# Preparing adj, weights and biases as pieces of the list schedule, in a four-layer graph network on one core

## The reference, cut to what matters

```python
x = layernorm(x + L0(x))   # D^-1/2 adj D^-1/2 (x @ w0) + b0, D = row sums of adj
x = layernorm(x + L1(x))   # 8-head attention masked by adj == 0; o = proj(...) + b; o + layernorm(o)
x = layernorm(x + L2(x))   # 3 GRU steps: a = adj @ h; z, r, candidate from a and h by w3, w4, w5, u3, u5
x = layernorm(x + L3(x))   # 8-head attention, scores + (1 - adj) * -1e9; Wq, Wk, Wv, Wo with biases
```

## Time and profile before

| | |
|---|---|
| device time, median of 3 runs | 2658.07 us (2657.05 to 2658.81) |
| device time of the profiled execution | 2658.25 us |
| its span in the trace | 2656.5 us |
| busy: PE, DVE, ACT, POOL | 97%, 74%, 72%, 27% of the span |
| granted TensorE clock, mean | 0.991 |
| HBM traffic | 14.36 MB read, 8.39 MB written |

### The profile page before, as it was taken

The page is one execution under the profiler, slowest core; times in us unless marked ns, Lnnn a source line. Parts: engine busy times, 40 slices in busy tenths (PEclk is TensorE's granted clock), DMA queues, the critical chain, the costliest instruction groups (busy, mean ns, idle before and its releaser), DMA issues.

```text
span 2656.5 us, 50191 instructions
## 1 busy us (share of the span) xinstructions
PE 2576.8 (97%) x17448; PEld 2056.3 (77%) x17448; DVE 1962.5 (74%) x5499; ACT 1904.9 (72%) x4284; POOL 715.1 (27%) x1065
## 2 busy tenths in 40 slices
PE   4999999999999999999999999999999999999997
PEld 3877877787877878778787787878777787777875
DVE  5867867868587786867768587685877868676776
ACT  2767947768587775858768587685867859574777
POOL 1222141322313222132322313223132321413221
PEclk7999999999999999999999999999999999999999
DMA  3312212122031221203122121221302113021122
GB/s 114 72 25 49 49 29 60 41 48 49 24 77 29 53 45 46 67 17 72 33 51 54 26 63 41 48 49 40 68 22 58 39 44 69 17 49 24 26 62 58
DMA packets 85081, 126.68 MB, mean 48 GB/s; under 512 B 15264, under 2 KB 34144, under 8 KB 84832
## 3 DMA queue, kind: packets, MB, share of 16 engines
q1 hardware_dynamic: 84832, 123.47, 19.7%
HBM read 14.36 MB, written 8.39 MB: 9 GB/s over the span
## 4 chain that ended last, share of the span: by engine, by line
PE 88%; DVE 6%; ACT 2%; issue 2%; POOL 1%; SPq 1%; DMA 0%; ACTq 0%; DVEq 0%; POOLq 0%
PE bank L1220 17%; PE bank L1222 17%; PE bank L1221 17%; PE bank L1279 15%; PE bank L1294 8%; PE bank L1271 8%; PE bank L1299 2%; PE bank L1262 2%; PE bank L1332 1%; PE bank L1239 1%; DVE probs L1028 1%; ACT probs L789 1%; SPq L616 1%; DVE PT L1039 1%; ACT PT L798 1%
## 5 line engine op out<-in xcount | busy, mean ns | idle before, releaser
L789 ACT ACTIVATE probs<-probs,few 128x512 f32<-128x512 f32 x1024 | 731.3, 718 | 90.1 <-DVE few L1028 86.5
L1028 DVE CUSTOM_DVE_ANT_0 probs<-bank,mask 128x512 f32<-128x512 f32 x1024 | 674.9, 683 | 61.0 <-PE bank L1279 26.0
L1279 PE MATMUL bank<-ident,probs 128*128 128x128 f32 x4096 | 588.6, 273 | 11.0 <-ACT probs L789 8.6
L1279 PEld LDWEIGHTS bank<-ident,probs 128*128 128x128 f32 x4096 | 483.9, 141 | 94.4 <-issue 25.4
L1271 PE MATMUL bank<-stack 96*128 96x512 f32 x1024 | 422.3, 453 | 0.7 <-DMA stack<-qk 0.5
L798 ACT ACTIVATE PT<-bank 128x512 f32<-128x512 f32 x640 | 360.0, 594 | 61.8 <-PE bank L1299 35.4
L1039 DVE COPY PT<-bank 128x512 f32<-128x512 f32 x384 | 262.8, 688 | 95.9 <-PE bank L1279 67.2
L709 POOL TENSOR_TENSOR feat<-o,feat 128x256 fp32r<-128x256 f32 x128 | 95.2, 744 | 632.7 <-ACT feat L811 614.8
L1220 PE MATMUL bank<-feat,W 128*128 128x512 f32 x640 | 258.6, 404 | 0.3
L1294 PE MATMUL bank<-PT,vh 128*32 128x256 f32 x4096 | 254.6, 383 | 2.5 <-DVE PT L1039 1.4
L1222 PE MATMUL bank<-feat,W 128*128 128x512 f32 x640 | 253.3, 396 | 0.0
(11 more groups left out here) (117 smaller groups left out, 5091.5 us busy)
## 6 DMA issues: line engine op xcount, KB each, us to landing
stack<-qk SPq DMA_DIRECT2D x768, 128.0 KB, 2.4
res<-in_x_dram SPq DMA_DIRECT2D x16, 512.0 KB, 3.8
out_dram<-res SPq DMA_DIRECT2D x16, 512.0 KB, 3.0
PT<-in_adj_dram SPq DMA_DIRECT2D x1, 1024.0 KB, 5.7
PT<-in_L_gnn_w_w_dram SPq DMA_DIRECT2D x2, 512.0 KB, 6.9
raw<-in_L_gnn_w_qkv_dram SPq DMA_DIRECT2D x1, 768.0 KB, 9.6
vh<-in_L_gnn_w_w_dram SPq DMA_DIRECT2D x1, 512.0 KB, 8.1
res<-in_L_gnn_u_w_dram SPq DMA_DIRECT2D x2, 256.0 KB, 8.1
```

The costliest lines, as they stand in the source:

```text
L789: k = act.activation(p, p, ACT.Exp, bias=least[:, t % P_RING:t % P_RING + 1], scale=-1.0, accum_out=sums[:, grp % 2, q * HG + h:q * HG + h ...
L1028: k = dve.tensor_tensor_reduce(out=probs[:, t % P_RING, :], in0=place("scores", t)[:, :], in1=mask[:, half * QT + q, :], scale=1.0, scalar ...
L1279: k = pe.transpose(place("transpose", t)[:, m * P:(m + 1) * P], probs[:, t % P_RING, m * P:(m + 1) * P], ident[:, :])
```

## The change

The preparation becomes pieces of the same scheduler, with nominal durations of their own (`PREP_US` and `RAW_US`), and each engine's stream is the list of its pieces from the first instruction on. The three waits for `bias31` go. In their place each consumer waits for what it reads: the first `ax` of a batch for the low part of adj, `w0` for its own weight, `q` and `k` for theirs, ScalarE's scaling for `dinv`. The load semaphore is split into seven. The one instruction for the plain weights on ACT and the one on DVE become three each (`w0`, `qkv1`, `rest`). SyncE loads adj, x of batch 0, w0, x of batch 1, the rows, wqkv, the GRU weights, the rest and the small biases; x of batch 2 waits until u3 and u5 are transposed, since those lie in its buffer. The first stacks of keys wait for the whole preparation, since `raw` now lies over `stack` and the first part of `PT` instead of `feat` and `qk`. The computation is the same.

```diff
+PREP_US = {"deg": 2.65, "mask1": 1.14, "mask3": 1.14, "dinv": 0.1, "pow": 0.8, "q1": 0.34, "q3": 0.34, "u5": 0.35,
+           "cols": 0.6, "bv": 0.6, "bo": 0.35, "to_rows": 0.12, "hi_qkv1": 1.35, "hi_rest": 2.2, "lo_qkv1": 1.65,
+           "lo_rest": 2.75, "bias": 1.2}
+RAW_US = {"adj": (0.6, 4.6), "w0": (0.6, 2.5), "rows": (1.8, 2.0), "qkv1": (0.6, 3.5), "gru": (3.0, 5.0), "rest": (3.0, 5.0),
+          "small": (6.0, 2.0)}
...
+    for name in ("adj", "x0", "w0", "x1", "rows", "qkv1", "gru", "rest", "small"):
+        add("first", "SP", ("load", int(name[1])) if name[0] == "x" else ("raw", name))
+    for m in range(NT):
+        add(("prep", "PE"), "PE", ("prep", "PE", adjs[m]), ("raw", "adj"), opens=[("adjT", m)])
+        add(("prep", "ACT"), "ACT", ("prep", "ACT", adjs[m]), ("prep", "PE", adjs[m]))
+        add(("prep", "DVE"), "DVE", ("prep", "DVE", adjs[m]), ("prep", "ACT", adjs[m]), frees=[("adjT", m)])
+    add("degrees", "DVE", ("prep", "DVE", "deg"), ("raw", "adj"))
+    add("degrees", "POOL", ("prep", "POOL", "pow"), ("prep", "DVE", "deg"))
+    add("degrees", "DVE", ("prep", "DVE", "dinv"), ("prep", "POOL", "pow"))
...
+    for loaded, scaled, name in (("w0", None, "w0"), ("qkv1", "q1", "qkv1"), ("rest", "q3", "rest")):
+        if scaled:
+            add("plain", "DVE", ("prep", "DVE", scaled), ("raw", loaded))
+        add("plain", "ACT", ("prep", "ACT", f"hi_{name}"), ("raw", loaded), *([("prep", "DVE", scaled)] if scaled else []))
+        add("plain", "DVE", ("prep", "DVE", f"lo_{name}"), ("prep", "ACT", f"hi_{name}"))
...
+        add("turned", "PE", ("prep", "PE", name), ready, opens=[("turn", name)])
+        add(("turned", "ACT"), "ACT", ("prep", "ACT", name), ("prep", "PE", name))
+        add(("turned", "DVE"), "DVE", ("prep", "DVE", f"lo_{name}"), ("prep", "ACT", name), frees=[("turn", name)])
...
+    prepared = [("prep", "DVE", name) for name in ("bias", "lo_u5", "mask3", "dinv", adjs[-1])]
...
-        add(sp, "SP", ("load", b), *([("store", b - STREAMS)] if b >= STREAMS else []))
+        if b >= 2:
+            add(sp, "SP", ("load", b), ("store", b - STREAMS) if b >= STREAMS else ("prep", "PE", "u5"))
         for t in range(NT):
-            add(act, "ACT", ("act", "scale", b, t), ("load", b))
+            add(act, "ACT", ("act", "scale", b, t), ("load", b), ("prep", "DVE", "dinv"))
...
-                    add(pe, "PE", ("pe", x_, b, layer, g), ("dve",) + xT + (FT - 1,), opens=[(x_, b, layer, g)])
+                    add(pe, "PE", ("pe", x_, b, layer, g), ("dve",) + xT + (FT - 1,), ("prep", "DVE", "lo_qkv1"),
+                        opens=[(x_, b, layer, g)])
...
+                        *(prepared if layer == 1 and b == 0 else []), *([("stt", last_of_head(first, h))] if first else []))
...
-        raw = nc.alloc_sbuf_tensor_at("raw", [P, FT, PLAIN], F32, offset=at)
...
+        at = nc.sbuf_base
...
-            sp.wait_ge(prep_dve.sem, prep_dve.at("bias31"))
...
+                    if b == 2:
+
+                        wait_full(sp, "turn", "u3")
+                        wait_full(sp, "turn", "u5")
...
+                    if layer == 1 and b == 0:
+
+                        sp.wait_ge(prep_dve.sem, len(prep_dve.steps))
...
-            act.wait_ge(prep_dve.sem, prep_dve.at("bias31"))
...
+                if b == 0 and t == 0:
+                    act.wait_ge(prep_dve.sem, prep_dve.at("dinv"))
...
-            pe.wait_ge(prep_dve.sem, prep_dve.at("bias31"))
...
+                    if f == 0 and b < STREAMS:
+                        pe.wait_ge(prep_dve.sem, prep_dve.all(adjs))
...
+                    if b < STREAMS:
+                        pe.wait_ge(prep_dve.sem, prep_dve.at("lo_w0"))
...
+                    if layer == 1 and b < STREAMS:
+                        pe.wait_ge(prep_dve.sem, prep_dve.at("lo_qkv1"))
```

More of the change, by code:

```diff
@@ L38, in at, with all @@
         return it * len(self.steps) + self.place[step] + 1
+    def all(self, steps):
+        return max(self.at(step) for step in steps)
     def raised_by(self, instruction, step):
@@ new lines, in adj_resnorm_kernel @@
+    add("biases", "DVE", ("prep", "DVE", "cols"), ("raw", "small"), ("raw", "rows"))
+    add("biases", "PE", ("prep", "PE", "bv"), ("raw", "small"), ("raw", "rest"), opens=[("bv", 0)])
+    add("biases", "DVE", ("prep", "DVE", "bo"), ("prep", "PE", "bv"), frees=[("bv", 0)])
+    split = [("prep", "DVE", f"lo_{name}") for name in ("w0", "qkv1", "rest")]
+    add("biases", "DVE", ("prep", "DVE", "to_rows"), *split)
+    add("biases", "ACT", ("prep", "ACT", "bias_hi"), ("prep", "DVE", "bo"), *split)
@@ L214, in adj_resnorm_kernel @@
+    add("biases", "DVE", ("prep", "DVE", "bias_lo"), ("prep", "ACT", "bias_hi"))
+    add("biases", "DVE", ("prep", "DVE", "hi_row"))
+    add("biases", "DVE", ("prep", "DVE", "bias"))
+    prepared = [("prep", "DVE", name) for name in ("bias", "lo_u5", "mask3", "dinv", adjs[-1])]
     for b in bs:
@@ L465, in adj_resnorm_kernel @@
         stored = [sem(f"stored{j}") for j in js]
[L466 to L469, removed]
+        adj_loaded, w0_loaded, rows_loaded, qkv1_loaded, gru_loaded, rest_loaded, small_loaded = (
+            sem(f"{name}_loaded") for name in ("adj", "w0", "rows", "qkv1", "gru", "rest", "small"))
         prep_pool = Signal(sem("prep_pool"), ["zero", "power", "one", "ident", "pow"])
[L471 to L476, removed]
+        parts_of = {"deg": ["sum", "least", "some"], "cols": ["bq", "z", "r", "c", "half"], "hi_row": ["hi_row1", "hi_row3"],
+                    "bias": ["bias10", "bias11", "bias30", "bias31"]}
+        prep_dve = Signal(sem("prep_dve"), [step for key in order.by_engine["DVE"] if key[0] == "prep"
+                                            for step in parts_of.get(key[2], [key[2]])])
+        prep_act = Signal(sem("prep_act"), [key[2] for key in order.by_engine["ACT"] if key[0] == "prep"])
         dve_mark = sem("dve_mark")
@@ L608, in adj_resnorm_kernel @@
         block = ctx.enter_context(nc.Block())
-        RAW_LOADS = 16 * (3 + 2 + 7 + 3 + 5 + 2 + 3)
+        SMALL = 16 * (2 + 5 + 3)
+        plain = {"w0": slice(0, col["q1"]), "qkv1": slice(col["q1"], col["o1"]), "rest": slice(col["o1"], PLAIN)}
         @block.sync
         def _(sp):
[L615 to L632, removed]
-            sp.wait_ge(prep_dve.sem, prep_dve.at("bias31"))
@@ L1336, in _ @@
             for key in order.by_engine["PE"]:
-                if key[0] == "scores":
+                if key[0] == "prep":
+                    prepare(key[2])
+                elif key[0] == "scores":
                     scores(key[1])
```

294 lines of the change are left out of this document (201 added, 93 removed).

## The result

The changed kernel takes 2644.36 us (median of 5, 2643.5 to 2646.49), the kernel before on the same chip 2658.81 (2657.05 to 2658.99): ratio 0.9949, 95% interval 0.9935 to 0.9964. That is 14.5 us won; 16.7 were forecast. The profiled execution took 2644.1 us with a span of 2642.3.

The account below looks back on a forecast made before the run. Other engines' chain sets a 49.4 us prologue, then TensorE sets the pace. The same TensorE work is through at 55.8 instead of 72.5 us, so 16.7 us are won: 2641.5 us, own range 2636 to 2648.

Parts of the forecast that it names:

- `ax` at 17.2: Prologue, TensorE's first matmuls of batch 0: start at 17.2 us instead of 49.4.
- `w0` 29.4: Prologue, batch 0: the w0 product runs from 29.4 to 32.2 us, after the transposes and the bias product.
- `q` 42.1: Prologue, batch 0: q starts at 42.1 us, after two evacuations on VectorE.
- First scores 55.8: End of batch 0's prologue: the first attention scores start at 55.8 us instead of 81.9.
- 16th group 318.6: Attention tiles: the 16th group ends at 318.6 us instead of 335.3, with the same distance to the end.
- the loads: DMA in the prologue: 0.37 MB per us after adj, rest in at 21.6 us, the last bias at 24.3.
- the +4 us that I had set aside as a bound: Prologue, TensorE: lower clock through the transposes and w0 would add 4 us.
- GpSimd's addition: Prologue, after x's split: GpSimd's addition of b0 holds VectorE up by 2.1 us, bounds 0 and 2.6.
- Tiles set the pace: Rival: attention tiles, not TensorE's total, set the pace, so all 26.1 us stay: 2632 us; chance 0.12.
- VectorE gives it back between the tiles: Rival: evacuations of batches 1 and 2 come between tiles, leaving a gain of 9 us: 2649 us; chance 0.17.
- Stacks wait: Rival: key stacks wait for the last preparation and stop TensorE's queue ahead of the scores: 2664 us; chance 0.04.
- It doesn't do what it says: Rival: VectorE's 24.6 us of preparation stay a block, total moves 0 to 5 us: 2656 us; chance 0.05.

Follow-up runs that it names:

- e10: The changed kernel with one scheduler number altered, the nominal landing of w0 after 6 us instead of 2.5: 2643.71 us.
- e1: The changed kernel, but x is split only when the whole preparation is done, so no batch work lies beside it: 2645.67 us.
- e6: As e1, but every piece of the preparation behind adj waits for the last load again, as before the change: 2653.88 us.
- e9: The changed kernel with one scheduler number altered, the nominal landing of the last weights (rest) after 12 us instead of 5: 2634.55 us.
- e3: The changed kernel with the scheduler's nominal issue and landing times of the loads replaced by those of its trace: 2629.02 us.
- e2: The changed kernel with x of batches 0 and 1 loaded behind all weights and biases: 2641.16 us.
- e7: The changed kernel with 48 transposes of the identity that nobody waits for, between the scores of tiles 80 and 81: 2648.34 us.
- e4: The changed kernel with 24 idle transposes behind w0 and 12 ahead of q, to keep TensorE's higher clock: 2644.51 us.
- e8: As e3, with 12 idle transposes among the transposes of the GRU weights and 12 ahead of q: 2627.96 us.
- e11: As e3, with wqkv loaded ahead of the rows and x of batch 1 behind the GRU weights: 2632.89 us.

## Why the prediction was right in size, and where its reasons failed

**The steps.** `ax` at 17.2: it was 16.9. w0 ahead of adj on ScalarE and VectorE cost more than said (VectorE's row sum began at 9.91, not 9.5), GpSimd's power less (1.03 us, not 2.22). `w0` 29.4: it was 31.3. `q` 42.1: 43.7. First scores 55.8: 56.8. 16th group 318.6: 319.9.

**The point up to which it was summed.** The prediction took the 16th group for the place from which the lists are the same. So does the part on the change, with "from tile 128 on". Both are wrong by one piece, 2.0 us of TensorE's work, and the good agreement at that group is in part luck. Where the lists do meet, the same forecast is 335.4 - 16.7 = 318.7, and it was 322.0. The gain runs so: 15.6 us at "ready" (81.7 - 66.1), 13.4 where the lists meet, 14.2 between the spans (2656.5 and 2642.3), 14.5 between the medians. So 1.1 of the 16.7 us were missing at "ready". The next 2.2 us went in the tiles, where the sum had carried everything on; pauses of TensorE are the same 5.6 us, and its lower clock from 129.6 to 136.4 us, which no term of the sum had, is the difference that the traces show. The 0.8 us that came back behind the meeting lie within the scatter there (2318.9 to 2321.8).

**The term that was mis-sized: the loads.** I had `rest` in at 21.6 us. VectorE waited for it until 24.36, 1.91 us, in front of the evacuation of `ax`. The rate in slices of 1.5 us, against the earlier trace rows:

```profile
GB/s 0 106 347 392 367 348 225 144 415 404 397 376 349 348 347 115 2 0 0 0 26 255 69 0 5 0 0 0 0 11 0 0 0 0 0 153 195 206 198 198
```

Two slices, 9 to 12 us, fall to 225 and 144 GB/s, while the rows are loaded. At 370 they would have carried 0.56 MB more, which is 1.5 of the 2.8 us; the others I can't place. So the last sum was done at 27.1 instead of 25.9, and the transposes of the GRU weights ran behind a pause of 1.88 us at 0.21 us each, the lower clock: part of the +4 us that I had set aside as a bound came. Fewer matmuls at the lower clock gave some back: `ax` had 8 at 0.43 us, `q` 9, where I took 12 for each. So part of the closeness of the first scores (1.0 us) is luck: a late load against a clock that rose sooner.

**GpSimd's addition.** I had it hold VectorE for 2.1 us, and looked for a VectorE instruction of 2.5 to 3.3 us right after the split; there was none. At first GpSimd waited: its addition started at 16.99, VectorE's mask and low part of wqkv ran at their usual 1.22 and 1.75 until 19.64, and the addition ended 2.25 us behind that, at 21.89 (in e10, where VectorE does nothing when it starts, it takes 2.38). Then VectorE waited: its sum, started at 20.27, ended 0.56 us behind the addition, 2.18 us instead of 0.69. That 1.5 us cost nothing on VectorE's way to the evacuation of `ax`, since VectorE then waited for `rest`. The Trainium skill (SBUF — State Buffer, section "Who interferes with whom") has the two exclude each other on a shared port pair, and lets the one that issues first keep it. The rows agree with that; the prediction gave only the case in which GpSimd is first.

**The step that failed: what the gain is made of.** The prediction put all of it on `ax` starting 32.2 us earlier, less 15.5 given back. e1 has nothing beside the preparation and wins 11.8 us; e6 shows that 8 to 9 of these come from starting on a weight when its own load is in. The overlap as scheduled nets 1.3 us in the medians, no more than the noise: 4.2 at "ready", 2.0 where the lists meet, 1.6 by the spans. The 2.2 lost between are those of the change's tiles, where e1's clock stays up. The count was right because it followed VectorE's list, which holds both effects; the story told over it was wrong. What should have warned me stands in the earlier trace rows: of 49.4 us VectorE worked 24.6, and it began on the weights only when the last load was in. A kernel that fills just these waits, and overlaps nothing, I never priced; in e1 its preparation ends at 36.3 us.

**The overlap's gain went into the table of landing times.** By it `rest` was due 7.8 us too early, so its pieces stood ahead of batch 0's on an engine that takes its instructions in order. One number (e9) gives back 9 to 10 us, the table as traced (e3) 15.

**The rivals.** *Tiles set the pace*: false. First scores 24.9 us earlier won 13.4 us where the lists meet. "Ready" to there stays at 253.7 us whether the first scores come at 65.4 (e2) or 81.7, and 4.2 of e7's 5.3 us stay. The Trainium skill (Perfetto Trace Analysis, section "Identifying the Most-Contended Engine") would take weight-load time, 78% here, beside the share of peak arithmetic as the measure of what TensorE has free, and not matmul busy time, 98% here; of the 5.3 us of inserted matmuls 4.2 stayed although 22% should have been free, so at this place the measurement stands against it. *VectorE gives it back between the tiles*: false, from 56.9 to 100 us TensorE works 43.09 of 43.10, and its pauses from there to 320.9 us are 5.6 us, as many as in before between 100 and 335.3. *Stacks wait*: not here; with the first scores or the clock ahead of them changed it begins to show (e4 0.30 us, e8 1.23, e9 1.46), and is the next thing in the way. *It doesn't do what it says*: half true. `q` did come earlier (43.7 us, where `ax` alone began at 49.4 in before), but most of that a shorter preparation gives by itself, and x loaded early won nothing over x loaded last.

## What to carry to other kernels

When work that stood in a block is mixed into a schedule, price the block by itself too: here four fifths of the gain came from reordering it by its loads, and only an experiment that kept the two apart showed it. A schedule made at build time puts its estimates into in-order queues, so a load that the table has in too early stops everything behind it; landing times are read from a trace of the kernel and put back into the table (0.9949 became 0.9890 here). Where one engine's total sets the pace, compare the work done at one point of its list, and check instruction by instruction that it is the same point in both: here it was off by 2.0 us. A difference won there was carried on whole where the order behind it was the same, and to within some 3 us where it was not.

## What was unexpected of the hardware

- GpSimd and VectorE each wait for the other's instruction to end. GpSimd's two-input addition over 128x1024 takes 2.38 us when it starts first (e10). It took 4.90 in the change, 4.72 and 3.85 in e3 and 6.36 in e11, where VectorE's masks and two-input work lay beside it, each time ending 2.2 to 2.3 us behind the last of them. The other way round VectorE's sum took 2.18 instead of 0.69, four of its splits 3.82 instead of 1.67 (e3), one split 2.60 (e9).
- The same shows in GpSimd's power over 128x4, which took 2.22 us in before and 1.03 in the change. In before it started at 9.05 us beside VectorE's first mask and ended at 11.27, when the second one did (before, first fence). In e6 it ended with the one mask beside it (second fence). In the change low parts of adj lay beside it, of which VectorE reads one operand from PSUM, and it did not wait.

```profile
10.01 1.22 DVE L923 TENSOR_SCALAR mask<-PT 128x2048 f32<-128x2048 f32 x1
```

```profile
8.66 1.68 POOL L749 TENSOR_TENSOR probs<-probs,few 128x4 f32<-128x4 f32 x1 [7.13 <-DVE probs L1018]
9.09 1.22 DVE L1024 TENSOR_SCALAR mask<-PT 128x2048 bf16<-128x2048 f32 x1
```

- The DMA rate fell from 350-390 to 225 and 144 GB/s for 3 us. In e2, where the rows stand two loads earlier in the queue, the two slow slices come 3 us earlier (247 and 184 GB/s from 6 to 9 us), which speaks for the rows; no run took them away.
